# Cross-attention and ffn layer on one core: scores computed twice, once for their maxima and once as keys by queries, with rows assembled by DMA through DRAM

## The reference

```
q = (layernorm(x) @ Wq + bq)          16 heads of 16
k, v = ctx @ Wk + bk, ctx @ Wv + bv
att = softmax(where(mask, scale * q.k, -1e10))       per head, over 77 keys
x = x + (att.v) @ Wo + bo
h = relu(layernorm(x) @ w1[0] + b1[0])               256 -> 1024
t = layernorm(x)
x = x + layernorm(t + h @ w2[0] + b2[0]) * gamma + beta
```

## Time and profile before

| what | value |
|---|---|
| median of three runs | 287.38 us (285.75 to 288.05) |
| the profiled execution, its time | 287.75 us |
| its span | 286.0 us |
| mean granted clock of TensorE | 0.92 |

### The profile page before, as it was taken

One profiled execution on the slowest core, in us unless ns is written; L12 is line 12 of the kernel. 1 busy time (PEld: TensorE's weight loads), 2 busy tenths in 40 slices (PEclk: granted clock), 3 DMA queues, 4 the chain that ended last, 5 costly groups with the idle time before them and its releaser, 6 DMA issues.

```text
span 286.0 us, 3844 instructions
## 1 busy us (share of the span) xinstructions
PE 217.4 (76%) x1321; PEld 166.9 (58%) x1321; DVE 208.0 (73%) x413; ACT 116.2 (41%) x193; POOL 110.4 (39%) x96
## 2 busy tenths in 40 slices
PE   0276928639476996497996988999799599978991
PEld 0244616315255874167785854779577457966891
DVE  0527789999775997948799982769999422878564
ACT  1041342942511686344202995541248453025700
POOL 0100316949201379611231399430328930136011
PEclk9999886957995999869997999999979979999998
DMA  6795000000000000000010100001000000101001
GB/s 187 210 322 168 2 1 0 0 0 1 2 0 0 2 1 0 0 2 0 0 39 0 37 2 3 0 2 37 0 11 28 0 2 0 40 0 37 1 21 55
DMA packets 8704, 8.68 MB, mean 30 GB/s; under 512 B 1479, under 2 KB 8429, under 8 KB 8685
## 3 DMA queue, kind: packets, MB, share of 16 engines
q1 hardware_dynamic: 6896, 7.43, 8.3%
q10 hardware_dynamic: 1789, 1.01, 1.3%
HBM read 6.34 MB, written 2.10 MB: 29 GB/s over the span
## 4 chain that ended last, share of the span: by engine, by line
DVE 35%; PE 26%; POOL 15%; issue 13%; ACT 7%; DMA 2%; ACTq 1%; POOLq 0%; DVEq 0%
PE W L462 5%; DVE mx L706 4%; POOL Pm L840 4%; DVE yb L799 4%; DVE dn L716 3%; POOL xn L854 3%; POOL x L854 3%; PE S L437 2%; DVE yb L804 2%; PE W L391 2%; POOL hl L860 2%; ACT hr L606 2%; DVE Pm L710 2%; PE W L515 2%; PE W L392 2%
## 5 line engine op out<-in xcount | busy, mean ns | idle before, releaser
L840 POOL TENSOR_TENSOR Pm<-Pm,rd 128x616 f32<-128x616 f32 x32 | 41.4, 1298 | 74.7 <-DVE rd L721 74.7
L512 PE MATMUL W<-w2h,hh 128*128 128x256 f32 x128 | 38.8, 303 | 0.0
L437 PE MATMUL S<-Kb,qs 128*128 128x308 f32 x128 | 29.5, 358 | 12.2 <-issue 9.4
L498 PE MATMUL W<-x2h,w1h 128*128 128x512 f32 x64 | 28.5, 446 | 13.1 <-ACT hr L606 6.5
L515 PE MATMUL W<-w2h,hl 128*128 128x256 f32 x128 | 36.2, 283 | 0.2 <-DVE hl L768 0.2
L513 PE MATMUL W<-w2l,hh 128*128 128x256 f32 x128 | 36.2, 283 | 0.0
L606 ACT ACTIVATE hr<-W,cols 128x512 f32<-128x512 f32 x32 | 22.0, 686 | 31.7 <-PE W L500 14.3
L449 PE MATMUL W<-cst,Pm 128*128 128x128 f32 (+1 forms) x160 | 23.7, 278 | 11.9 <-DVE qs L658 9.0
L437 PEld LDWEIGHTS S<-Kb,qs 128*128 128x128 f32 x128 | 22.0, 215 | 17.6 <-issue 16.9
L578 ACT ACTIVATE Pm<-Pm 128x616 f32<-128x616 f32 x32 | 23.0, 719 | 21.9 <-DVE Pm L710 21.6
L449 PEld LDWEIGHTS W<-cst,Pm 128*128 128x128 f32 (+1 forms) x160 | 18.6, 140 | 17.9 <-DVE qs L658 10.4
(11 more groups left out here) (96 smaller groups left out, 446.9 us busy)
## 6 DMA issues: line engine op xcount, KB each, us to landing
xin<-in_x_dram SPq DMA_DIRECT2D x4, 512.0 KB, 9.3
out_dram<-yb SPq DMA_DIRECT2D x6, 256.0 KB, 2.2
xn<-in_L_ffn_w_dram SPq DMA_DIRECT2D x1, 1024.0 KB, 5.0
x<-in_L_ffn_w_dram SPq DMA_DIRECT2D x1, 1024.0 KB, 7.6
out_dram<-yb SPq DMA_DIRECT2D x4, 128.0 KB, 1.7
hr<-in_mask_1x1xSxS_fk_dram ACTq DMA_DIRECT2D x1, 308.0 KB, 7.6
wq<-in_L_xattn_Wq_dram SPq DMA_DIRECT2D x1, 256.0 KB, 4.4
wo<-in_L_xattn_Wo_dram SPq DMA_DIRECT2D x1, 256.0 KB, 7.1
```

Of the source, the lines that this page charges most:

```text
L437: e.matmul(s[:, h, 0:4 * TK], qs[:, 2 * g + h, n * 128:(n + 1) * 128], Kb[:, 2 * g + h, w, :], start=(w == 0), stop=False)
L498: e.matmul(t[:, :], w1h[:, o:o + 128], x2h[:, k, :], start=(k == 0), stop=False)
L512: e.matmul(y, hh[:, f, q:q + 128], w2h[:, f * E:(f + 1) * E], start=(f == 0), stop=False)
L840: e.tensor_tensor(p3, p3, rd[:, u, :].unsqueeze(2).to_broadcast([P, 8, TK]), ALU.mult).then_inc(weighted, 1)
```

## The change

Nothing stays of the common list: each engine now has a list of its own, made from the table TIMES, which gives every step a number to sort by (`walk(engine)`). Each engine goes through its list strictly in order. Chunks now alternate between the batches: (batch 0, first half), (1, first), (0, second), (1, second); so chunks 0 and 1 share the first 512 mask rows and chunks 2 and 3 the second 512.

Scores are computed twice.

- `smax` (48 steps, two matmuls each): queries by keys from stacked operands `Mq` and `KM`. Mq has in rows 0 to 76 the turned mask, in 77 and 78 a flag for the query bias, from 79 on three heads' high queries; KM has an identity under the mask rows and the keys in a block pattern. 462 or 308 columns per step go to a reduce on VectorE. The maxima of the chunk are turned (`mxt`), negated and written to DRAM (`nD`).
- `st` (64 steps, one 512-column matmul each): keys by queries, from `KS` and `Sq`. Sq has the same 79 mask and flag rows, then 16 rows of high queries twice and of low queries once, and the negated maximum as row 127. So the result needs only an exponential to be the turned weight (`PT`), with no transposes, subtraction, sum or scaling.
- `pv` (16 steps, four heads at once): `Vb` has a column of ones, so the sums come with the weighted values. The result goes to DRAM (`pD`), is gathered as numerators and sums, the sums are inverted, go to DRAM (`rD`) and come back spread over 16 rows a head; VectorE multiplies (`attn`).

The keys, queries, biases and maxima reach their rows in KM, KS, Mq and Sq by DMA from DRAM. The mask rows come by these copies: ACT issues the first three as soon as the mask is turned, SP the last two at "maskm" and "masks".

The names: `QR` is 79, `KP` 78, `NC` 4, `CHUNKS[c]` the batch and half of chunk c. The table entries around them:

```diff
+    "PE": {
+        "smax": ("31.3 31.5 ... 40.5 / 45.0 ... 55.1 / 64.3 65.5 ... 74.6 / 79.6 ... 96.8"),
+        "st": ("47.7 ... 61.4 / 67.7 ... 83.3 / 89.4 89.7 ... 123.7 / 125.1 ... 161.0"),
+        "proj": "84.7 / 117.9 / 149.4 / 183.4",
+        "turn2": "94.7 / 129.3 / 162.8 / 195.8",
+        "ffn1": ("99.2 ... 109.5 / 133.6 ... 144.4 / 167.7 ... 179.7 / 199.7 ... 210.0"),
...
+    "SP": {
+        "maskm": "55.4",
+        "masks": "83.7",
```

Where a row has "...", entries are left out here. The steps:

```diff
+        Mq = sb("Mq", [P, 6, 512], F32R)
+        Sq = sb("Sq", [P, 8, 512], F32R)
...
+            mT = early("mT", [QR, 1024], F32R)
...
 scalar_program
+                elif kind == "mask":
+                    e.wait_ge(mT_made, 1)
+                    first = mT[:, 0:512].bitcast(F32)
+                    e.dma_start(Mqf[0:QR, :, :], first.unsqueeze(1).to_broadcast([QR, 6, 512])).then_inc(ms_static, 16)
+                    e.dma_start(Sqf[0:QR, :, :], first.unsqueeze(1).to_broadcast([QR, 8, 512])).then_inc(sq_static, 16)
+                    e.dma_start(mD[:, :], mT[:, :].bitcast(F32)).then_inc(m_out, 16)
...
 sync_program
+                elif kind == "maskm":
+                    e.wait_ge(m_out, 16)
+                    e.wait_ge(scored, 24)
+                    e.dma_start(Mqf[0:QR, :, :], mD[:, 512:1024].unsqueeze(1).to_broadcast([QR, 6, 512])
+                                ).then_inc(ms_static, 16)
+                elif kind == "masks":
+                    e.wait_ge(m_out, 16)
+                    e.wait_ge(st_made, 32)
+                    e.dma_start(Sqf[0:QR, :, :], mD[:, 512:1024].unsqueeze(1).to_broadcast([QR, 8, 512])
+                                ).then_inc(sq_static, 16)
+                elif kind == "qproj":
+                    e.wait_ge(q_high, nth[step])
+                    e.dma_start(qD[c][0, g * P:(g + 1) * P, :], qh[:, g, :].bitcast(F32)).then_inc(q_out[g], 16)
+                    e.wait_ge(q_split, nth[step])
+                    e.dma_start(qD[c][1, g * P:(g + 1) * P, :], ql[:, g, :].bitcast(F32)).then_inc(q_out[g], 16)
...
+                elif kind == "quadq":
+                    for r, l in ((0, 0), (1, 0), (2, 1)):
+                        q = QR + D * r
+                        e.dma_start(Sqf[q:q + D, s:s + 4, :], qq[l]).then_inc(sq_ld[u % 2], 16)
...
+                elif kind == "pv":
+                    e.dma_start(pD[c][4 * k:4 * k + 4, :, :], pvq[:, u % 2, :]).then_inc(pv_out[u % 2], 16)
+                elif kind == "gather":
+                    e.wait_ge(pv_out[0], 16 * (2 * c + g + 1))
+                    e.wait_ge(pv_out[1], 16 * (2 * c + g + 1))
+                    e.dma_start(den[:, g, :], pD[c][8 * g:8 * g + 8, D, :].rearrange("h (a n) -> h a n", n=32)
+                                ).then_inc(den_ld[g], 16)
+                    e.dma_start(num[:, g, :], pD[c][8 * g:8 * g + 8, 0:D, :]).then_inc(num_ld[g], 16)
...
+                elif kind == "spread":
+                    e.dma_start(rsB[:, :], rD[c][8 * g:8 * g + 8, :].unsqueeze(1).to_broadcast([8, D, 512])
+                                ).then_inc(rsb_ld, 16)
...
 tensor_program
+                elif kind == "smax":
+                    e.wait_ge(ms_ld, 32 * (c + 1))
+                    e.wait_ge(ms_static, 16 * (c // 2 + 1))
+                    e.wait_ge(keys_ld[b], 160)
+                    if nth[step] > 2:
+                        e.wait_ge(maxed, nth[step] - 2)
+                    w, r = (3, 127) if s < 2 else (2, 111)
+                    for j in range(2):
+                        i = e.matmul(m[:, j * w * KP:(j + 1) * w * KP], Mq[0:r, 2 * s + j, n * 128:(n + 1) * 128],
+                                     KM[0:r, b, h0:h0 + w, :].rearrange("p h t -> p (h t)"), start=True, stop=True)
...
+                elif kind == "st":
+                    e.wait_ge(sq_ld[u % 2], 64 * (u // 2 + 1))
+                    e.wait_ge(sq_static, 16 * (c // 2 + 1))
+                    e.wait_ge(keys_ld[b], 160)
+                    if nth[step] > 2:
+                        e.wait_ge(exped, nth[step] - 2)
+                    e.matmul(T[(nth[step] - 1) % 2][0:TK, :], KS[:, b, h, :], Sq[:, h % 8, :],
+                             start=True, stop=True).then_inc(st_made, 1)
+                elif kind == "pv":
+                    for j in range(4):
+                        i = e.matmul(acc[32 * j:32 * j + 32, :], Vb[:, b, 4 * k + j, :], PT[:, (4 * u + j) % 6, :],
+                                     start=True, stop=True, tile_position=(0, 32 * j))
```

More of the change, by code:

```diff
@@ L21 @@
 TK = 77
+KP = 78
+QR = 79
 F = 1024
[L23 to L26, removed]
 EPS = 1e-5
 BIG = float(2.0 ** 60)
[L29 to L130, removed]
-            if c == 0:
-                plans.append(spread(b[2], b[3], [("split", w, k) for w in (1, 2) for k in range(4)]))
-                plans.append([(b[4], ("xbias", 0)), (0.3, ("splitwo",))])
-            if c:
-                plans.append(spread(b[2], b[3], [("ffn1", c - 1, f) for f in range(8)]))
-                plans.append([(b[4], ("bias2", c - 1))])
-            if c + 1 < NC:
-                if c + 2 < NC:
-                    plans.append([(a[6], ("norm", c + 2))])
-                plans.append([(b[5], ("turn", c + 1)), (b[6], ("qproj", c + 1, 0)), (b[7], ("xbias", c + 1))])
-            weave(*plans)
-    for f in range(8):
-        put("ffn1", NC - 1, f)
-        tick()
-    drain()
-    for h in range(2):
-        for part in range(4):
-            put("ffn2", NC - 1, h, part)
-            tick()
-    drain()
-    return order
@@ new lines, with ordinals @@
+KINDS = ("consts", "ctx", "rows", "crow", "kproj", "bqk", "mask", "values", "keys", "split", "splitwo", "maskm",
+         "masks", "norm", "scale", "turn", "xbias", "qproj", "qload", "smax", "mxt", "quadq", "quadm", "st", "pv", "gather",
+         "invert", "spread", "attn", "alow", "proj", "scale2", "turn2", "bias2", "ffn1", "low", "ffn2", "result", "root",
+         "finish")
+def ordinals():
+    return {step: n + 1 for kind in KINDS for n, step in enumerate(s for row in members(kind) for s in row)}
@@ L286, in build @@
         bank, free_when = {}, {}
-        idle = [(W[k], None) for k in range(3)]
+        idle = [(w, None) for w in W]
         def occupy(key):
             bank[key], free_when[key] = idle.pop(0)
-        for step in order:
+        ends = {}
+        for row in members("result"):
+            for step in row:
+                c, h, na, nb = step[1:]
+                ends["ffn2", c, h, 2 * nb - 1] = nth[step]
+        for step in walk("PE"):
             kind, a = step[0], step[1:]
             n = nth[step]
-            if kind == "rows":
-                occupy(step)
-                idle.append((bank[step], (cols_made, 1)))
-            elif kind in ("turn", "turn2"):
+            if kind in ("turn", "turn2"):
                 for k in range(2):
@@ L317, in build @@
                     free_when[step] = None
-            elif kind == "result":
-                c, h, na, nb = a
-                idle.append((bank["ffn2", c, h, 2 * nb - 1], (y_made, n)))
+                if step in ends:
+                    idle.append((bank[step], (y_made, ends[step])))
         def wview(w):
@@ L446, in tensor_program @@
                     t = take(step)
                     for n in range(4):
[L448 to L464 removed]
+                        i = e.transpose(t[0:H, n * 128:(n + 1) * 128], mx[:, n, :], ident)
@@ L612, in vector_program @@
         def vector_program(e):
-            for step in order:
+            for step in walk("DVE"):
                 kind, a = step[0], step[1:]
```

712 lines of the change are left out of this document (427 added, 285 removed), and 89 rows, old and new, of the table TIMES.

## The result

| | before | after |
|---|---|---|
| median | 287.56 us (285.75 to 288.05) | 437.14 us (435.69 to 437.78) |
| ratio to before | | 1.521 [1.514, 1.529] |
| span of the profiled execution | 286.0 us | 434.8 us |

The account below looks back on a forecast made before the run. Before, two nearly full engines, TensorE and VectorE, handed work to each other. After, single-engine mask copies decide: 254 us until the last, 135 of remaining TensorE work and 9 to the end give 398 of span, 400 us; range 355 to 440.

Parts of the forecast that it names:

- The savings: Engine work removed: VectorE some 50 us less, GpSimd 41.4, TensorE 15 to 20, ScalarE even.
- One engine for 79 rows: Mask copies: 79 is prime, so one DMA engine moves each whole copy, at 24.5 GB/s.
- A: First Mq copy, which the first smax awaits: start 21, plus 39.6 and 11 us of sharing, ends at 71.6 us.
- B: First Sq copy, which the first st awaits: 52.8 plus 4 us, ends at 128.4; smax and maxima's trip hidden in it.
- sharing term: Time SP's transfers take on the mask copies' one engine: 11, 4, 2, 1 and 1 us over the five copies.
- C: Copy of mD from mT, plus 2 us: ends at 142.4; SP waits for it at maskm.
- D: SP's Mq copy at maskm for the second half: 39.6 plus 1 us, ends at 183; chunk 2's first smax waits.
- The weights of chunk 1: After chunk 2's first smax: 16 exponentials, 4 copies and one trip of about 4 us, 17 us, until 200.
- E and the rest: SP's Sq copy at masks, 52.8 plus 1 us, ends at 254; then 135 us of TensorE with idle, 9 to the end.
- Neither bounds: Trips through DRAM: 178 issues, 66 us of SP, and 23 MB, 64 us of all engines, both beside other work.
- The first one: Rival: mask copies spread over the engines, all their waits vanish, 230 us (223 to 236), faster; chance 9%.
- The second: Rival: copies quick, but trips exposed in every chunk, 21 us for each of three later chunks, 293 us; chance 4%.

Follow-up runs that it names:

- the best version: Query rows in Sq and KS interleaved three apart, against the kernel with copies split and behind the queries, maxima stored by ACT: 278.8 us, 0.969.
- the seven sizes: A kernel of DMAs alone, copies of 128, 80, 79, 78, 77, 76 and 64 rows one after another: 40.5 us at 79 rows, 6.3 to 11.7 otherwise.
- The splits: The changed kernel with mask copies issued as 64 and 15 rows: all five 282.5 us, only ACT's three 359.3, only SP's two 359.9.
- the experiment's expectation: Expectation for the changed kernel with all five mask copies issued as 64 and 15 rows: 246 us; measured 282.5 us, 0.979.
- a new order: Split copies with maxima stored by ACT (284.0 us), now Sq and mD copies behind chunk 0's queries and batch 1's keys loaded later: 281.1 us, 0.973.
- GpSimd's issue: The changed kernel with the second and third 79-row copies issued by GpSimd instead of ACT: 437.7 us, 1.519.

## Why the prediction was right, point by point

**The savings** were right in sign: TensorE fell by 11 us (15 to 20 forecast), GpSimd by 35 (41), VectorE by 69 (50). ScalarE stayed even, as forecast; VectorE's size was off most, by 19 us. None reached the time while the copies stood in the way; with the copies in parts, 5 us of 287 did, and 9 in the best version.

**One engine for 79 rows** was right. The end marks counted in the context load gave the rule, and the seven sizes confirm it. The rate was 25.6 GB/s for the 24.5 taken, 4% less time per copy.

**A and B, the start.** The step that failed is "smax, the turned maxima and their trip are hidden in it". The copies themselves were through at 69.2 and 122.3 us, 2 and 6 earlier than forecast, since hardly a transfer of SP shared the engine. But nothing was hidden behind them: ACT stood in its issues until 111.7, and the whole start, 40 us of it, came after. The first st was at 151.6 instead of 128.4: 23 us of the 37 missed. The forecast had no term for the time that an engine stands in an issue. Nor was its sharing term large enough. With ACT's copies later in its list, start and copies did run side by side, and the first st came with Sq's copy at 137.6, 9 us later than forecast; with a third queue on the engine it came at 153.9.

**C and D.** C was not on the path. mD's copy was through at 137.9, and SP came to `maskm` only at 160.5, with its own list, so it didn't wait for C as the forecast said. D took 45.6 us to its end mark (160.6 to 206.2) where the forecast had 40.6: once SP's stall was over, at 193, its other transfers had their shares on the same engine. The first smax of chunk 2 came at 207.9 (183 forecast). Against the forecast, measured from the first st, C is 5 us less and D with the last load into Mq 7 us more, so that the sum of both is off by only 2 us. That is luck.

**The weights of chunk 1** are the second term that was too small: from 207.9 to 239.9 it is 32 us, where 17 stood for 16 exponentials, 4 copies and one trip. That adds 15 us. SP's stall behind copy D is not the reason, for the stretch takes 31.8 us in the kernel where SP doesn't stand there, and 31 to 34 in every version but the one with fewer loads, where it takes 27.4. The DMA engines were 63% busy from 199 to 240 us, and TensorE worked at a granted clock of 0.62; how much each adds stays open.

**E and the rest.** From 239.9 to 294.2 it is 54.3 us (53.8 forecast), from there to the end 140.6 (144 forecast). The sum of the misses is 23 + 2 + 15 + 0.5 - 3.4, 37 us: the whole difference. The range held because its upper end had 21 us for chunk 1 and fuller sharing. The stall was not among its terms, and 3 us more would have left the range, so that it held is partly luck.

**The signs named beforehand.** Long waits before the first smax and the first st of chunk 2, copies that take 35 to 60 us, a DMA share near 1/16 and a first ffn1 after 250 us (306.7) were all seen. One sign of being wrong was half met as well: "another wait" ends most of TensorE's idle time. Of the 179 us in the three gaps, 92 ended with ACT's stalled issues and not with a DMA into Mq or Sq. The splits show that the 79 rows are behind this gap too.

**"Neither bounds", of the trips' bytes and issues,** is wrong: chunk 1's 15 us are a stretch in which the copies hid nothing, and with the copies in parts, fewer loads gained 11 us. At 361 GB/s the 23 MB were 64 us of the engines, but that rate was read from loads that fill all rows. Into 16 neighbouring rows it is 96 to 118.

**The rivals.** The first one, copies spread over the engines, can be tried by splitting them, and gives 282 us where I had put 230 (and 246 in the experiment's expectation). The second, trips exposed in every chunk, 293, was nearer in its number; leaving out loads, with every trip's steps in place, gained 11 us of it. Of the 36 us between 246 and 282.5, these 11 are shown, and a new order brought 1, less than the intervals resolve. Among the rest are the two copies of SP in parts, 12 us each from issue to the matmul behind them, though 4 and 6 us of TensorE's idle time. The granted clock is 0.57 to 0.87 in the five stretches above, so TensorE's own work is longer there too. How the remaining 24 us divide between these copies, the loads that remain, this clock and the order of the trips was not separated.

## What to carry to other kernels

Before a DMA is costed by its bytes, count how many engines its rows give (largest divisor up to 16) and which rows it writes: 79 rows took 40.5 us where 80 took 7.1, and 16 rows side by side cost 2.6 times the engine time of 16 rows seven apart. A transfer on few engines costs three times: its own time, the time its issuing engine stands in the next issue, and a delay of every transfer that has a share on the same DMA engine. Where several causes stand one behind the other, taking the front one away (GpSimd's issue, the new order) shows little; take all away first, then look at what is left. And a cause read from one trace needs a second kernel without it: SP's stall stood right before the long stretch of chunk 1, and the stretch stayed as long without the stall.

## What was not expected of the hardware

The issue of a DMA stood 32 to 50 us when the DMA before it in the same queue had 79 rows, on ACT, on SP, and in a kernel with nothing else. It ended 7 to 8 us before the end mark of a copy that had the engine to itself (124.1 against 131.5, 61.2 against 69.2), so the wait is not for the whole copy. Three queues on one DMA engine had 72 packets each in 20 us, of 4,096, 2,048 and about 1,000 B on average. A packet of 2,048 B took 80 ns on an engine alone and 283 ns when sixteen engines wrote 16 neighbouring rows.
